# Attention with a tanh gate: head groups in pairs, copies moved to ScalarE, and values ahead of keys and queries

## What is computed

```python
h = _layernorm(x, axis=-1) * (1 + ca) + sa
x_norm = _layernorm(h, gamma, beta)
q, k = l2_normalize(heads(x_norm @ w_q)), l2_normalize(heads(x_norm @ w_k))
v = heads(h @ w_v)
align = einsum('bhqd,bhkd->bhqk', q, k)
resonance = 0.5 + 0.5 * tanh((align - 0.27) * 15.0)
gate_q = 0.25 + 0.75 * sigmoid(q @ g_q)
gate_k = 0.25 + 0.75 * sigmoid(k @ g_k)
fused = einsum('bhqk,bhkd->bhqd', resonance * gate_q * gate_k, v)
x = x + ga * (fused @ w_o + b_o)
```

## Time and profile before

| | us |
|---|---|
| median of 3 runs (1297.47 to 1300.64) | 1300.12 |
| profiled execution, its own time | 1298.31 |
| span from its first to its last instruction | 1296.5 |
| first attention, 41 to 388 us: length | 347.0 |
| TensorE busy in it (mean granted clock 0.99 of full speed) | 333.9 |
| VectorE busy | 316.4 |
| ScalarE busy | 315.2 |
| GpSimd busy | 170.0 |

### The profile page before, as it was taken

The page is one execution under the profiler, slowest core; times in us unless marked ns, Lnnn a source line. Parts: engine busy times, 40 slices in busy tenths (PEclk is TensorE's granted clock), DMA queues, the critical chain, the costliest instruction groups (busy, mean ns, idle before and its releaser), DMA issues.

```text
span 1296.5 us, 36994 instructions
## 1 busy us (share of the span) xinstructions
PE 1207.8 (93%) x13717; PEld 808.7 (62%) x13717; DVE 1046.9 (81%) x2935; ACT 929.8 (72%) x1338; POOL 573.2 (44%) x793
## 2 busy tenths in 40 slices
PE   3899999999997899996999999999789999999998
PEld 2555555555544667774555555555368888888876
DVE  5899999999967787757899999999556777777763
ACT  0699999999993565542788888888657676776775
POOL 2455555555522243323343334334146565565653
PEclk7799999999999999998999999999979999999999
DMA  5411111111102122102000000000000000000000
GB/s 136 151 35 36 38 38 37 38 38 38 30 10 58 47 57 59 44 19 82 31 15 15 18 14 15 18 15 14 7 1 10 9 17 9 17 17 10 17 9 27
DMA packets 48061, 41.91 MB, mean 32 GB/s; under 512 B 5377, under 2 KB 46689, under 8 KB 47361
## 3 DMA queue, kind: packets, MB, share of 16 engines
q1 hardware_dynamic: 47872, 39.45, 10.7%
HBM read 35.09 MB, written 4.34 MB: 30 GB/s over the span
## 4 chain that ended last, share of the span: by engine, by line
PE 48%; DVE 3%; issue 1%; ACT 0%; POOL 0%; DVEq 0%; POOLq 0%
PE psum_all L2821 24%; PE psum_all L2356 9%; PE psum_all L2342 4%; PE psum_all L2123 2%; PE psum_all L2382 2%; PE psum_all L2319 1%; PE psum_all L2328 1%; PE psum_all L2368 1%; PE psum_all L2309 1%; PE psum_all L2868 1%; PE psum_all L2374 1%; PE psum_all L2115 0%; PE psum_all L2683 0%; DVE ffn_gated L2977 0%; DVE ffn_xhat L2674 0%
## 5 line engine op out<-in xcount | busy, mean ns | idle before, releaser
L2443 ACT ACTIVATE a_probs<-psum_all 128x1024 f32<-128x1024 f32 x256 | 248.2, 1023 | 68.0 <-PE psum_all L2342 67.9
L2821 PE MATMUL psum_all<-ffn_hi,weights_r 128*128 128x512 f32 x704 | 283.5, 403 | 8.9 <-issue 3.6
L688 ACT ACTIVATE probs<-psum_all,biases 128x1024 f32<-128x1024 f32 x256 | 270.4, 1114 | 25.5 <-PE psum_all L594 25.5
L2821 PE MATMUL psum_all<-ffn_lo,weights_r 128*128 128x512 f32 x704 | 278.2, 395 | 0.0
L2785 POOL TENSOR_TENSOR ffn_lo<-ffn_full,ffn_hi 128x512 fp32r<-128x512 f32 x143 | 185.0, 1302 | 132.2 <-ACT ffn_hi L2898 99.2
L2821 PEld LDWEIGHTS psum_all<-ffn_hi,weights_r 128*128 128x128 f32 x704 | 134.4, 191 | 45.8 <-DVE ffn_full L2982 8.9
L2821 PEld LDWEIGHTS psum_all<-ffn_lo,weights_r 128*128 128x128 f32 x704 | 134.6, 191 | 26.2
L607 PE MATMUL psum_all<-probs,vpad 128*32 128x257 f32 x2048 | 138.0, 387 | 0.3 <-ACT probs L688 0.3
L2356 PE MATMUL psum_all<-a_probs,vpad 128*32 128x256 f32 x2048 | 137.6, 386 | 0.6 <-DVE a_sums L2521 0.6
L2910 ACT ACTIVATE ffn_full<-psum_all,scales 128x512 f32<-128x512 f32 x128 | 88.2, 689 | 68.6 <-PE psum_all L2821 68.5
L2785 DVE TENSOR_TENSOR ffn_lo<-ffn_full,ffn_hi 128x512 fp32r<-128x512 f32 x64 | 54.6, 853 | 79.7 <-ACT ffn_hi L2913 79.7
(11 more groups left out here) (232 smaller groups left out, 2641.2 us busy)
## 6 DMA issues: line engine op xcount, KB each, us to landing
a_mod_gate<-modulation_table SPq DMA_DIRECT2D x64, 128.0 KB, 2.9
X<-in_x SPq DMA_DIRECT2D x32, 128.0 KB, 3.2
a_mod_norm<-modulation_table SPq DMA_DIRECT2D x32, 128.0 KB, 3.0
f<-in_f SPq DMA_DIRECT2D x2, 2048.0 KB, 10.3
e_mod_norm<-modulation_table SPq DMA_DIRECT2D x32, 128.0 KB, 3.1
out<-X SPq DMA_DIRECT2D x16, 256.0 KB, 2.3
e_gates<-modulation_table SPq DMA_DIRECT2D x32, 64.0 KB, 2.8
weights<-in_h SPq DMA_DIRECT2D x2, 1024.0 KB, 7.8
```

Of the source, the lines that this page charges most:

```text
L688: nc.scalar.activation(probs[:, c % 4, :, :, 0:T].rearrange("p r k q -> p (r k) q"), SC[c % 2].rearrange("p (a q) -> p a q", q=T), ACT.Tan ...
L2443: nc.scalar.activation(probs[:, c % 4, :, :, :].rearrange("p r k q -> p (r k q)"), SC[c % 2], ACT.Exp, scale=float(np.float32(1.0) / np.sq ...
L2821: ins = nc.tensor.matmul(dst, weights[:, w0:w0 + P], part[layer][:, k, :], start=first and i == 0, stop=last and i == len(parts) - 1)
```

## The change

It has these parts, all in `attention_0` but for the tiles' sizes:

1. `heads` goes in pairs. In step b groups 0 and 1 of batch b run behind scores 6 and 7, and groups 2 and 3 behind scores 2 and 3 of step b+1. `probs` has 8 slots for it and `vpad` three buffers, and a tanh waits for the group of the batch before.
2. On TensorE, `project_out` moves from the end of the step to its beginning, one batch later; `turn_keys`, `turn_queries`, `turn` and `turn_gates` stand together ahead of scores 6. `turn_queries` writes into the bank of gates and output (`PG16`), no longer into `PT`, so `turn_gates` waits for the copy of the queries, and `turn` for the values, the logits and the copy of the keys.
3. `split_high` moves from VectorE to ScalarE, behind the last tanh of the step, as does `gT_out`; `split_low` and `double_keys` move into VectorE's next step.
4. The gates: two tanh, one for keys and one for queries, the latter spread straight over the channels; the affine part for queries is done by `gT_out` (an Identity with scale and bias in place of a copy). The gates come behind the second tanh, the squares behind the first.
5. Biases are constants in the instruction and no longer columns of a tile.
6. VectorE's order is written anew, with `values` and `logits_out` ahead of the Newton steps and of both copies; `stats_1` and `norm_1a` work one batch further ahead.
7. GpSimd: `modulate`, `double_queries`, second root, `gate_out`, first root; `gate_out` waits for `xn` as well.

```diff
-                    wait(pe, qT_done, n - 1)
+                    wait(pe, values_done, n - 1)
+                    wait(pe, logits_done, n)
+                    wait(pe, kT_done, n - 1)
...
                 def turn_queries(n, p):
-                    pe.wait_ge(kT_done, n + 1)
                     pe.wait_ge(query_stacked, n + 1)
+                    wait(pe, x_done, n - 2)
+                    wait(pe, gT_done, n - 1)
...
                 def turn_gates(n, p):
                     pe.wait_ge(gates_done, n + 1)
-                    wait(pe, gT_done, n)
+                    pe.wait_ge(qT_done, up_to(n + 2))
...
+                    if there(b):
+                        scores(b, p, 0)
+                        scores(b, p, 1)
...
+                    if there(b + 2):
+                        project_qk(b + 2)
+                    if there(b + 2) or there(b + 1):
+                        project_logits_v(b, p)
+                    if there(b - 2):
+                        project_out(b - 2, p)
+                    if there(b):
+                        scores(b, p, 2)
+                        scores(b, p, 3)
+                    if there(b - 1):
+                        heads(b - 1, 1 - p, 2)
+                        heads(b - 1, 1 - p, 3)
...
+                    if there(b):
+                        scores(b, p, 4)
+                        scores(b, p, 5)
+                    if there(b + 1):
+                        turn_keys(b + 1, 1 - p)
+                        turn_queries(b + 1, 1 - p)
+                    if there(b + 3) and b != -1:
+                        turn(b + 3)
+                    if there(b):
+                        turn_gates(b, p)
+                    if there(b):
+                        scores(b, p, 6)
+                        scores(b, p, 7)
+                        heads(b, p, 0)
+                        heads(b, p, 1)
...
                 def gate(n, p):
...
+                    nc.scalar.activation(tanh_k[:, :].rearrange("p (t v) -> p t v", t=TT), by_kind[:, :, 1, :],
+                                         ACT.Tanh, scale=0.5 / SPLIT_SCALE).then_inc(tanh_k_done, 1)
                     wait(act, gates_psum, n - 1)
+                    nc.scalar.activation(tanh_q[p][:, :, :].rearrange("p t (v d) -> p t v d", d=HD),
+                                         by_kind[:, :, 0, :].unsqueeze(3).broadcast_to([P, TT, H, HD]), ACT.Tanh, scale=0.5 / SPLIT_SCALE)
+                    act.wait_ge(tanh_k_done, n + 1)
                     wait(act, values_done, n)
+                    nc.scalar.activation(gate_k[:, :], tanh_k[:, :], ACT.Identity, bias=gate_k_bias, scale=0.375).then_inc(gates_done, 1)
...
-                        if c == 0 and there(b + 1):
+                        if c == 0 and there(b + 2):
+                            square(b + 2)
+                        if c == 1 and there(b + 1):
                             gate(b + 1, 1 - p)
-                        if c == 1 and there(b + 2):
-                            square(b + 2)
-                        if c == 5 and there(b):
-                            gT_out(b)
+                        if c == CHUNKS - 1:
+                            if there(b):
+                                gT_out(b)
+                            if there(b + 2):
+                                split_high(b + 2, p)
...
                 def gate_out(n, p):
                     pool.wait_ge(mod_gate_loaded[p], n * 8 + (16 - 8 * p))
+                    pool.wait_ge(xn_done, up_to(n + 4))
...
```

More of the change, by code:

```diff
@@ L328, in attention_0 @@
     nw = [sb(f"newton{i}", [P, 64]) for i in range(6)]
-    logits, gate_in, gate_tanh = sb("logits", [P, 64]), sb("gate_in", [P, 64]), sb("gate_tanh", [P, 2, TT, H])
-    gate_k, gate_q = sb("gate_k", [P, TT * H]), [sb(f"gate_q{i}", [P, TT, D]) for i in range(2)]
+    logits, gate_in, gate_k = sb("logits", [P, 64]), sb("gate_in", [P, 64]), sb("gate_k", [P, TT * H])
+    tanh_k = sb("tanh_k", [P, TT * H])
+    tanh_q = [sb(f"tanh_q{i}", [P, TT, D]) for i in range(2)]
     stack = [sb(f"stack{i}", [P, 2, TT * H, 4, HD], F16) for i in range(2)]
@@ L863, in step @@
                 def step(b, p):
-                    older, old, new, next_, turns = there(b - 2), there(b - 1), there(b + 1), there(b + 2), there(b + 3)
-                    ahead = turns and not (isinstance(b, int) and b == -3)
+                    older, old, new, next_ = there(b - 2), there(b - 1), there(b + 1), there(b + 2)
+                    turns, fresh = there(b + 3), there(b + 4)
+                    ahead = turns and b != -3
                     def newton_of(*ks):
@@ L872, in step @@
                     if ahead:
[L873 to L881 removed]
+                        norm_1b(dve, b + 3)
+                    if new:
+                        split_low(b + 1, 1 - p)
+                        double_keys(b + 1, 1 - p)
+                    if next_:
+                        square_sums(b + 2)
+                    if ahead:
+                        stats_2(dve, b + 3, 0)
+                        stats_2(dve, b + 3, 1)
                     if new:
[L883 removed]
+                        values(b + 1)
                     if next_:
@@ L3099, in sb0 @@
                     return part.enter_context(nc.sbuf_tensor(name, shape, dt))
-                sbuf["vpad"] = [sb0(f"vpad{i}", [P, TT, H, 32]) for i in range(2)]
-                sbuf["probs"] = sb0("probs", [P, 4, 2, TT, UNIT_PAD])
+                sbuf["vpad"] = [sb0(f"vpad{i}", [P, TT, H, 32]) for i in range(3)]
+                sbuf["probs"] = sb0("probs", [P, CHUNKS, 2, TT, UNIT_PAD])
                 sbuf["wqk0"], sbuf["wv0"], sbuf["wo0"] = sb0("wqk0", [P, 2 * D]), sb0("wv0", [P, D]), sb0("wo0", [P, D])
```

153 lines of the change are left out of this document (52 added, 101 removed).

## The result

| | us |
|---|---|
| changed kernel, median of 4 runs (1322.88 to 1325.53) | 1324.35 |
| kernel before, median of the 4 runs beside them (1297.47 to 1303.00) | 1300.38 |
| ratio, with its 95% interval | 1.0179 (1.0154 to 1.0204) |
| profiled execution after: own time, span | 1325.53, 1323.4 |
| VectorE's `oT` product to the next, after and before | 11.65, 10.87 |

The kernel is 1.8% slower; 1323 was forecast, in a range of 1299 to 1335. Over 107 to 319 us every engine is busy for less of the time than before. The windows view gives it, the kernel before first, then the changed one; after the window and its length each column is an engine's busy time and its instructions (TensorE, its weight load, VectorE, ScalarE, GpSimd), then TensorE's granted clock, the DMA share and GB/s.

What follows compares the result with a forecast made beforehand. VectorE was taken as the bound, 10.5 us of work in a 10.87 us step. Six items sum to a ring of 11.67, +0.80 over 31 steps, +24.8 on 1298.3: forecast 1323 us, range 1299 to 1335.

Steps and rivals of the forecast that it cites:

- item: One of six stretches of the loop of waits through one step: 3.06, 2.02, 1.84, 1.34, 0.75 and 2.66 us.
- holding or none: VectorE, `xn` to `kT`: Newton 5 and 6 held until GpSimd's `x_biased` ends, 1.84 us, or not held, 1.25.
- the tanh at 0.92 or 1.00 back to back: ScalarE: each tanh 0.92 us with a constant bias, or 1.00 if the constant saves nothing.
- the ring: Loop of waits through ScalarE, VectorE, GpSimd and TensorE in each first-attention step, claimed to set it at 11.67 us.
- item 3: VectorE from `xn` to `kT`, with Newton 5 and 6 held beside GpSimd's `gate_out`: 1.84 us.
- The load of VectorE: VectorE's work per first-attention step after losing the cast, the hole and one Newton product's stretching: 9.67 us.
- A: First attention: Newton 5 and 6 slip past GpSimd without holding; 11.08 us a step, 1305 us; chance 0.12.
- C: ScalarE: the constant bias saves nothing on the tanh; 12.0 us a step, 1333 us; chance 0.04.
- B: First attention: engine loads decide, not the ring; step falls to about 9.9 us, 1268 us; chance 0.13.

Runs made afterwards that it cites:

- the two kernels above whose clock stayed at 1.00: Changed kernel with `gate_out` waiting for the keys' copy, 1309.58 us; changed kernel with Newton 5 and 6 behind the copies and last step's first head group earlier, 1295.33 us.

## Why the prediction was right, point by point

**The step.** 11.67 against 11.65, and no item off by more than 0.07. The two items that rested on choices between bounds were run by themselves: holding or none (1.84 or 1.25; measured 1.88, and 11.09 a step with GpSimd out of the way), and the tanh at 0.92 or 1.00 back to back (0.38 a step for the four with a tile, 0.33 estimated). That the ring decides and not the loads was tested from the other side: shortening item 3 by 0.97, by order alone, shortened the step by 0.95.

**The sum over the steps held, but partly because errors cancelled, and that is luck.** Forecast: 31 x 0.80 = 24.8. The medians differ by 24.0, the spans of the profiled executions by 26.9:

| stretch of the profiled executions | before | after | difference |
|---|---|---|---|
| first to last tanh of the stage | 346.7 | 368.5 | +21.8 |
| last tanh to the experts' first product | 5.8 | 9.2 | +3.4 |
| from there to the second attention's first tanh | 219.1 | 221.4 | +2.3 |
| the rest (with 0.1 ahead of the stage) | 724.9 | 724.3 | -0.6 |

The first term is 2.4 below 31 x 0.78 = 24.2: the last three steps take 29.4 us against 29.2 before, hardly more. With the turns absent there, ScalarE's wait for scores is 0.93 and 0.95 ahead of tanh 6 and 0.85 ahead of tanh 4 of the last step, instead of 1.98. The prediction counted all 31 steps alike.

The second and third terms the prediction had at nothing. For the second, the sentence at fault is "groups 0 and 1 run behind scores 6 and 7, long after their tanh, so I count them at nothing; if that cover went, a wait for the last tanh, at most one of 0.92". The cover does go in the last step: two head groups and an output projection stand behind the last tanh in place of one head group. At full clock that takes 7.7 us (the two kernels above whose clock stayed at 1.00), 1.9 more than before; the other 1.5 are the clock. The third term is the lower clock at the experts' start, whose cause is open. It is also why the prediction's own sign, "All of it is wrong if the three stages behind the first attention change by more than 1 us", was given by a forecast that was right: a stage behind did change by more, but not by anything in the forecast.

**What would show it.** `oT` products 11.5 to 11.8 apart: 11.65. ScalarE idle 1.5 to 2.2 ahead of one tanh in eight: 1.98; and ahead of tanh 4, 0.3 for 0.5. `turn` waits for `kT`: 1.45; `turn_gates` stands behind that and follows `qT`'s end (226.78) by 0.10. Newton 6 at 0.5 to 0.8: 0.65. Tanh 1.02: median 1.03. No hole ahead of `xhat`: right. VectorE idle ahead of `values`: only 0.20, which the view calls "issue", though it starts 0.09 behind `gate_k`'s end (233.24).

**What was missed on the way.** `values` had almost come free of `gate_k`. A second path, cast, `split_low`, `double_keys`, sums of squares, second statistics, is only 0.2 us shorter, so with a faster ring it is soon as long (11.09 with the gates' work moved, where VectorE has no gap left): `split_low` waits 0.38 for the cast, and both it and the copy behind it are held beside GpSimd's modulation (0.98 for 0.69, 0.71 for 0.29 before). The load of VectorE, forecast at 9.67, left these holds out and is too low: it is busy for 196.8 of 212 us, 10.8 of 11.65.

**The rivals.** A and C were the runs with the gates' work moved and with the tile (11.09 and 12.03 a step, forecast 11.08 and 12.0). B, loads decide, did not happen in this order. In the old order, with cast and constants, three engines are nearly full, at 10.41 and not at 9.9: TensorE's work there is 10.3 (209.0 of 212) and was put too low from its waits; which engine sets the step no run shows. One sum under B is wrong: the loads decide only once `values` to the last copy has shrunk from 5.2 to about 3.4 (11.67 less 1.77 is 9.9). At 4.4, as the prediction has it, the ring would be 10.87, the step of before.

## What to carry to other kernels

- Where engines run in program order, lay out the loop of waits through all of them before adding up loads, and sum it from start to start. Then keep off it whatever nobody on it reads: here two small Newton steps ahead of the two copies that the loop needed, with GpSimd's work beside them, cost 25 us.
- Relieving the fullest engine pays only down to the next one. Cast and constants gave 1.3 and 1.2 us alone, which is within the noise, and 14.3 together; try such pairs together before dropping either.
- A steady-state sum says nothing of the last steps. Look at what stands behind the last instruction of the engine that sets the end, and read TensorE's granted clock there. Before an edit gets the credit for a clock that stays up, look whether it stays up in a kernel without the edit: here it did, and the path was no shorter with the edit.
- An idle time says where a ring passes; look at the next waits on the same engine before naming the one that closes the new ring.

## What the runs showed of the hardware

- **VectorE and GpSimd hold each other up, and also where VectorE copies.** `double_keys`, a copy of one 16-bit tensor of SBUF to another, takes 0.29 us before and 0.71 beside GpSimd's products of the modulation. In the kernel with Newton behind the copies it takes 0.70, and GpSimd's first product, started 0.11 behind VectorE's `split_low`, takes 1.17 for 0.73. Timelines of VectorE and GpSimd there:

```profile
216.56 0.69 DVE L819 TENSOR_TENSOR a_stack<-a_qkn,a_stack 128x512 f16<-128x512 f32 x1
217.29 0.70 DVE L824 COPY a_stack<-a_stack 128x512 f16<-128x512 f16 x1
```

```profile
216.67 1.17 POOL L416 TENSOR_TENSOR a_scaled<-a_xhat,a_mod_norm 128x256 f32<-128x256 f32 x1 [1.01 <-DVE a_xhat L448]
```

  The one that starts second ends late: GpSimd's product at 217.84, 0.59 behind `split_low`'s end (217.25), and the copy at 217.99, 0.15 behind GpSimd's. The Trainium skill (SBUF — State Buffer, Who interferes with whom) says that a VectorE instruction with two SBUF inputs contends with a GpSimd one that reads SBUF, and so does a copy in a mode that uses both ports. The trace agrees on the first; the copy's 0.70 for 0.29 fits the second, though no row names its mode.
- **TensorE's granted clock can fall at the end of a stage whose mean is 0.99, and one trace doesn't say why.** It fell to 0.56 in the changed kernel's last step, where 32 products took 3.32 us for 1.94, and stayed at 1.00 in a kernel with the same order and the same gaps. At the start of the next stage it was 0.56 to 0.76 in seven of ten kernels, at 1.3 to 2.9 us. In the kernel with cast and constants it was 0.71 there, so some 2 us may be left in it (an estimate from the table above); that wasn't tried.
